# Four attention layers: a new step form for layer 4, reordered loads at each layer's head, moved splits in the middle loops

## The reference, cut to what matters

```python
x = layer0(x, ctx)   # 8 heads of 128: self attention, norm, cross attention, norm, feed-forward, norm
x = layer1(x, ctx)   # 16 heads of 16: self attention (mask), cross attention, feed-forward, three norms
x = layer2(x, ctx)   # as layer1, other mask and weights
# layer3:
q = (x @ Wq.T + bq).reshape(B, 128, 16, 16)
k = (ctx @ Wk.T + bk).reshape(B, 128, 16, 16)
v = (ctx @ Wv.T + bv).reshape(B, 128, 16, 16)
att = softmax(einsum('bhqd,bhkd->bhqk', q, k) / sqrt(16))
out = x + (einsum('bhqk,bhkd->bhqd', att, v) @ Wo.T + bo)
out = layer_norm(out) * gamma + beta
```

## Time and profile before

| | us |
|---|---|
| median of 3 runs | 3384.29 (3381.09 to 3385.19) |
| the profiled execution | 3386.52 |
| its span | 3384.8 |
| PE busy | 3052.0 |
| DVE busy | 2036.9 |
| ACT busy | 1909.7 |
| POOL busy | 1491.7 |
| SP's first load of cross / middle / fourth | 615.29 / 1454.23 / 3021.05 |

### The profile page before, as it was taken

The page is one execution under the profiler, slowest core; times in us unless marked ns, Lnnn a source line. Parts: engine busy times, 40 slices in busy tenths (PEclk is TensorE's granted clock), DMA queues, the critical chain, the costliest instruction groups (busy, mean ns, idle before and its releaser), DMA issues. The chain is left out here.

```text
span 3384.8 us, 82099 instructions
## 1 busy us (share of the span) xinstructions
PE 3052.0 (90%) x28400; PEld 2668.3 (79%) x28400; DVE 2036.9 (60%) x4306; ACT 1909.7 (56%) x7826; POOL 1491.7 (44%) x1874
## 2 busy tenths in 40 slices
PE   7999999599999999727999999999999999848886
PEld 5999998379999999625888888888888888745664
DVE  2545554244444444325777777888878778726665
ACT  2444444234444444325777777777777777617775
POOL 1223423103445444611555555555555555543444
PEclk8999999799999999858999999999999999979998
DMA  3222121410111110032222222333211121122321
GB/s 104 63 75 68 62 93 38 143 35 29 54 53 53 53 35 28 35 117 82 77 74 71 73 73 70 91 95 111 64 61 61 61 62 56 33 81 83 88 88 57
DMA packets 218094, 232.77 MB, mean 69 GB/s; under 512 B 41920, under 2 KB 183232, under 8 KB 215360
## 3 DMA queue, kind: packets, MB, share of 16 engines
q1 hardware_dynamic: 217920, 230.49, 21.6%
HBM read 148.57 MB, written 65.01 MB: 63 GB/s over the span
## 5 line engine op out<-in xcount | busy, mean ns | idle before, releaser
L1736 ACT ACTIVATE middle_stage<-middle_psum,middle_neg_max 128x128 f32<-128x128 f32 x2048 | 728.0, 392 | 344.6 <-DVE middle_neg_max L1716 344.4
L1736 ACT ACTIVATION_READ_ACCUMULATOR middle_stage<-middle_psum,middle_neg_max 128x1 f32 x2048 | 473.4, 231 | 0.0
L1716 DVE TENSOR_REDUCE middle_neg_max<-middle_psum 128x4 f32<-128x512 f32 x512 | 338.1, 682 | 64.9 <-PE middle_psum L1679 63.2
L1690 PE MATMUL middle_psum<-middle_eye,middle_stage 128*128 128x128 f32 x2048 | 320.5, 279 | 18.6 <-DVE middle_stage L1722 8.6
L1690 PEld LDWEIGHTS middle_psum<-middle_eye,middle_stage 128*128 128x128 f32 x2048 | 231.2, 142 | 72.0 <-issue 46.4
L1645 POOL TENSOR_TENSOR middle_attended_lo<-middle_mix,middle_attended_hi 128x256 fp32r<-128x256 f32 x128 | 95.0, 742 | 433.9 <-DVE middle_attended_hi L1728 433.9
L536 POOL TENSOR_TENSOR cross_ff_hidden_lo<-cross_ff_relu,cross_ff_hidden_hi 128x256 fp32r<-128x256 f32 x128 | 100.9, 789 | 279.9 <-DVE cross_ff_hidden_hi L531 279.9
L97 PE MATMUL middle_psum<-middle_n_yt_hi,middle_w_lo 128*128 128x256 f32 x640 | 193.7, 303 | 14.1 <-ACT middle_n_y L1853 12.5
L1946 POOL TENSOR_TENSOR middle_ff_hidden_lo<-middle_ff_relu,middle_ff_hidden_hi 128x256 fp32r<-128x256 f32 x256 | 183.4, 737 | 49.0 <-DVE middle_ff_hidden_hi L1940 49.0
L1722 DVE COPY middle_stage<-middle_psum 128x512 f32<-128x512 f32 x256 | 175.6, 686 | 15.6 <-PE middle_psum L1690 15.3
L1617 ACT ACTIVATE fourth_stage<-fourth_psum,fourth_neg_max 128x128 f32<-128x128 f32 x512 | 182.1, 387 | 3.4 <-DVE fourth_neg_max L1593 3.4
(11 more groups left out here) (346 smaller groups left out, 10915.8 us busy)
## 6 DMA issues: line engine op xcount, KB each, us to landing
middle_stage<-middle_a_k SPq DMA_DIRECT2D x1024, 16.0 KB, 1.8
middle_xt_hi<-x_hi SPq DMA_DIRECT2D x32, 256.0 KB, 2.7
middle_xt_lo<-x_lo SPq DMA_DIRECT2D x32, 256.0 KB, 3.0
middle_ct_hi<-context_hi SPq DMA_DIRECT2D x32, 256.0 KB, 2.9
middle_ct_lo<-context_lo SPq DMA_DIRECT2D x32, 256.0 KB, 3.2
middle_x_rows<-x_rows SPq DMA_DIRECT2D x32, 256.0 KB, 2.8
middle_mask_flags<-flags SPq DMA_DIRECT2D x128, 64.0 KB, 1.9
x_rows<-middle_n_z SPq DMA_DIRECT2D x32, 256.0 KB, 2.2
```

Of the source, the lines that this page charges most:

```text
L1690: ins = pe.transpose(banks.psum[:, TURN_BANK, x * SEQ:(x + 1) * SEQ], self.sh.p_wide[:, 4 * b + t, x, :], self.sh.eye[:])
L1716: dve.tensor_reduce(self.sh.neg_max[:, 4 * b + t, :], psum[:, SCORE_BANKS[t], :].rearrange("p (x k) -> p x k", x=4), AX_X, ALU.max, negate ...
L1736: ins = act.activation(self.sh.p_wide[:, 4 * b + t, x, :], psum[:, SCORE_BANKS[t], x * SEQ:(x + 1) * SEQ], ACT.Exp, bias=self.sh.neg_max[: ...
```

## The change

In words. (1) `phase8`: SP loads the first fold's operands, p_turned before arena, then the columns; v_row and rows come later. PE waits for the columns only ahead of its first bias sum and later for `bias_sums_read` in place of `biases`. In self ACT splits x(0) after the first fold, and POOL does its x split ahead of its wait for `biases`. In cross the two feed-forward pieces go to a buffer of their own (`late`, on y_rows and z2) and are split in round 0 behind heads 3 and 5. (2) Heads of the 16-head phases: the first piece is cut in two halves of 1024 columns; x, columns and further pieces are loaded in the order of need; in middle ACT splits pieces 0 and 1, copies k and q, then splits the rest; each k is spread as soon as its block is cleared. (3) Middle's loops: norm 2's high part is made by DVE, ACT's spread of x1 moves behind the exponentials of group 3, and DVE's norm of x1's first batch moves behind the last turned copy. (4) `phase16_last` uses `AttendWide`: one batch's sixteen heads at a time, in half steps; high parts by DVE; k is projected and spread two steps ahead; x, context are loaded three steps ahead, v's product goes to `FF_BANK`.

```diff
@@ phase8, SP
-            sp.dma_start(col[:], cols).then_inc(small_loaded.sem, 16)
-            sp.dma_start(v_row[:], v_row_dram.broadcast_to([P, H8 * DK8])).then_inc(small_loaded.sem, 16)
-            sp.dma_start(row[:].rearrange("p n f -> p (n f)"),
-                         rows.rearrange("(o n) f -> o (n f)", o=1).broadcast_to([P, len(names) * DM])) \
-              .then_inc(small_loaded.sem, 16)
             for i in range(n_big):
                 if i == 2:
+                    sp.dma_start(v_row[:], v_row_dram.broadcast_to([P, H8 * DK8])) \
+                      .then_inc(row_table_loaded.sem, 16)
...
                     load_round(0)
-                if 2 <= i < 5:
+                if 2 <= i < 4:
                     sp.wait_ge(folded.sem, i - 1)
-                elif i >= 5:
-                    sp.wait_ge(lo_made.sem, 4 * 3 + i - 4)
+                elif i == 5:
+                    sp.wait_ge(lo_made.sem, 14)
                 at = 3 * 512 + i * STAGE_COLS
-                half = slice((i % 2) * STAGE_COLS, (i % 2 + 1) * STAGE_COLS)
-                sp.dma_start(stage[:, half], packed[:, at:at + STAGE_COLS]) \
-                  .then_inc(stage_loaded[i].sem, 16)
                 if i < 3:
                     sp.dma_start(inner[:, i % 2, :], packed[:, i * 512:(i + 1) * 512]) \
                       .then_inc(stage_loaded[i].sem, 16)
+                sp.dma_start(staged(i), packed[:, at:at + STAGE_COLS]) \
+                  .then_inc(stage_loaded[i].sem, 16)
+                if i == 0:
+                    sp.dma_start(col[:], cols).then_inc(cols_loaded.sem, 16)
@@ phase8, ACT and DVE, one_round
+                    if cross and not post and h in (3, 5):
+                        weight_hi(4 + (h - 3) // 2)
...
+                    if cross and not post and h in (3, 5):
+                        weight_lo(4 + (h - 3) // 2)
@@ phase8, PE
-            pe.wait_ge(small_loaded.sem, 16 * 3)
...
-            pe.wait_ge(biases.sem, 1)
+            pe.wait_ge(bias_sums_read.sem, 1)
@@ phase8, POOL
-            pool.wait_ge(biases.sem, 1)
...
             make_flags(0)
+            pool.wait_ge(biases.sem, 1)
             one_round(0, False, False, True)
@@ phase16_full, ACT, x1
                     norm2.act(act, Back(r, 2), psum)
-                    norm2.act_hi(act, Back(r, 2))
-                spread(x1)
                 exp(x1_next, 2)
...
                 exp(x1_next, 3)
+                spread(x1)
@@ phase16_full, ACT, head
-            act.wait_ge(layer.lo_made.sem, layer.slots)
+            for s in range(2):
+                layer.act_piece(act, s)
+            act.wait_ge(layer.biases.sem, 1)
             proj1.act_k(act, 0, psum)
             proj1.act_q(act, 0, psum)
+            for s in range(2, layer.slots):
+                layer.act_piece(act, s)
+            act.wait_ge(layer.lo_made.sem, layer.slots)
@@ phase16_full, DVE, x1
                 if ok(-2):
+                    norm2.dve_hi(dve, Back(r, 2))
                     norm2.dve_lo(dve, Back(r, 2))
+                turned(x1[1], 3)
                 norm(x1[0])
-                turned(x1[1], 3)
@@ phase16_last, SP
-                    after, before, loaded = near(r, i, 1), near(r, i, -2), near(r, i, 2)
-                    if after:
-                        after[0].proj.sp_k(sp, after[1])
+                    keys, loaded, before = near(r, i, 2), near(r, i, 3), near(r, i, -2)
                     if loaded:
-                        loaded[0].sp_context(sp, loaded[1], ctx_t, tokens(r, i, 2))
-                        loaded[0].sp_x(sp, loaded[1], x, tokens(r, i, 2))
+                        loaded[0].sp_x(sp, loaded[1], x, tokens(r, i, 3))
+                    if keys:
+                        keys[0].proj.sp_k_chunk(sp, keys[1], 0)
+                    if loaded:
+                        loaded[0].sp_context(sp, loaded[1], ctx_t, tokens(r, i, 3))
+                    if keys:
+                        keys[0].proj.sp_k_chunk(sp, keys[1], 1)
+                        keys[0].sp_rows(sp, keys[1], x, tokens(r, i, 2))
@@ phase16_last, PE, one step
+                    if here:
+                        here[0].att.pe_scores(pe, here[1], banks, 1)
+                    turn(here, 0, 0)
+                    if before:
+                        before[0].att.pe_mix(pe, before[1], banks, 1)
+                    turn(here, 0, 1)
+                    if after:
+                        project_q(after)
+                    turn(here, 0, 2)
+                    turn(here, 0, 3)
+                    if before:
+                        before[0].att.pe_out(pe, before[1], banks, before[0].norm.sum_ready)
+
+                    if after:
+                        after[0].att.pe_scores(pe, after[1], banks, 0)
+                    turn(here, 1, 0)
+                    if keys:
+                        project_k(keys)
+                    turn(here, 1, 1)
+                    if here:
+                        here[0].att.pe_mix(pe, here[1], banks, 0)
+                    turn(here, 1, 2)
+                    if after:
+                        after[0].proj.pe_v(pe, after[1], banks, after[0].ct)
+                    turn(here, 1, 3)
@@ phase16_last, DVE, first half of one step
+                    inverse(here, 0)
+                    maximum(here, 1, 0)
+                    turned(here, 0, 0)
+                    maximum(here, 1, 1)
+                    norm(before, 1)
+                    turned(here, 0, 1)
+                    maximum(here, 1, 2)
+                    maximum(here, 1, 3)
+                    turned(here, 0, 2)
+                    turned(here, 0, 3)
```

404 lines of the change are left out of this document (207 added, 197 removed).

## The result

The changed kernel takes 3374.03 us (median of 16 runs), the kernel before 3384.62 (16 runs): ratio 0.9968, 95% interval 0.996 to 0.9976. It is faster, by 10.6 us (0.3%). The forecast was 3330, 3304 to 3357, so the direction came true and the size did not: a fifth of the expected 54 us. The profiled execution of the changed kernel took 3374.15 us.

What follows compares the result with a forecast made beforehand. Bounds: idle PE at the heads, PE in middle's loops, a chain across engines in fourth's. Terms -8.9 - 3.9 - 20 + 5 - 26.7 = -54.5 from 3386.5 give 3332.0, less 2.2: 3329.8, said 3330; range 3304 to 3357.

Steps and rivals of the forecast that it cites:

- Fourth's term, -26.7: Fourth's head and loop: 0.7 us gained at the head, 26 in the loop by shorter steps of two batches.
- Self's head, -8.9: Start of self: first fold 4 us sooner by load order, attention 4.7 us sooner by POOL's earlier x split.
- Cross's head, -3.9: Start of cross: 9 us off the head, 5.2 us added in round 0 by the moved weight splits.
- The 4 us at the fold: Start of cross: first fold's operands loaded first, so the fold was to start 4 us sooner, as in self.
- The two terms of the swap: Cross's feed-forward splits moved into round 0: idle 5.01 us off the head, 5.2 us added in round 0.
- Middle's head, -20: Start of middle: halved first piece, earlier x and k copy bring the first scores near 1481 in place of 1501.7.
- Middle's loops, +5: Middle's rounds: PE's 0.72 us wait for ACT goes, a 1.1 us wait for DVE's copy comes; layer 1 cancels.
- Rival (a): Middle's loops: norm and moments fit in DVE's idle times, -21 us in place of +5, total 3304; chance 0.2.
- The step of 18.1: Fourth's loop: a wide step of two batches takes 18.1 us in place of 19.98, bound by ACT's chain.
- my SP chain: Fourth's loop: SP's 16 DMAs with two loads between land 17.8 us into the step, so SP nearly binds.
- rival (c): Fourth's loop: less busy PE loses its clock, each step +5 us or more, total 3426; chance 0.05.
- rival (b): Fourth's loop: the wide step is no faster, as reading PSUM isn't sped up; total 3356; chance 0.15.

Runs made afterwards that it cites:

- experiment 4: Changed kernel with the starting semaphore increments of each phase dealt out to PE, ACT and POOL in thirds: 3361.9 us, 0.9933 of the kernel before.
- m_spread_only: Changed kernel with norm 2's high part in middle put back on ACT, late spread and norm kept: 3395.0 us, 1.0024 of the kernel before.
- f_store_early: Changed kernel with fourth's store of two steps back issued by SP ahead of k's spread: 3371.3 us, 0.9951 of the kernel before.
- experiment 7: Changed kernel with cross's two feed-forward pieces split before round 0 again, new load order kept: 3376.0 us, 0.9968 of the kernel before.
- m_all_back: Changed kernel with middle's loop order put back (high part on ACT, spread and norm at old places): 3352.8 us, 0.991 of the kernel before.
- m_hi_only: Changed kernel with middle's spread and DVE's norm put back, norm 2's high part kept on DVE: 3332.6 us, 0.9838 of the kernel before.
- combo3: Changed kernel with middle's spread and norm put back, starting increments shared by PE, ACT and POOL, fourth's store ahead of k's spread: 3313.2 us, 0.9783 of the kernel before.

## Why the prediction was wrong, step by step

**The step that failed most.** Fourth's term, -26.7, came at -7.4: its loop was taken to be bound by ACT's chain alone, and falls of PE's clock, SP's store and a longer head and tail had no price in it. The second is middle's, -20 + 5 together, where PE's start and the chain to the maximum were wrong: +6.6. The direction came true, the size only by a fifth.

**Self's head, -8.9: -8.3 measured, in part for other reasons.** The fold started at 9.59 and not 4 us sooner, at 6.7; experiment 4 shows that PE's increments held it, since with a third of them it starts at 6.46. POOL's split off the path came true: attention starts 5.8 us sooner, at 49.0. The other 2.5 us lie elsewhere, and a difference of this size says little. Self is the same code in eight of the profiled kernels, and took 602.0 to 613.1 us. Most of that is there at the first maximum already, at 54.18 us in the shortest (`m_spread_only`) and 62.08 in the longest (`f_store_early`); the time between the later maxima is the same to 0.2 us. What differs in the head is the clock. The window from 30 to 62 us in the shortest, the longest, the changed kernel and the kernel before:

```profile
30.00:62.00 32.00, 29.37 (x148) 21.11 (x149) 14.37 (x22) 8.89 (x18) 5.27 (x5) 1.00 0.22 74
```

```profile
30.00:62.00 32.00, 30.43 (x124) 19.67 (x124) 11.80 (x18) 7.27 (x10) 0.00 (x0) 0.89 0.16 58
```

```profile
30.00:62.00 32.00, 30.50 (x135) 21.12 (x134) 12.69 (x20) 8.04 (x17) 2.46 (x4) 0.89 0.16 58
```

```profile
30.00:62.00 32.00, 25.86 (x97) 16.77 (x96) 9.25 (x14) 6.72 (x9) 6.87 (x3) 0.79 0.18 57
```

So the same code at the same place had the clock at 1.00 or at 0.89, and -8.3 and -3.2 of single executions can't be told from values some us away.

**Cross's head, -3.9: -3.2, by luck.** The 4 us at the fold didn't come: its first matmul stands 9.67 us after SP's first load and stood 9.82 before, with 63 increments ahead of it. The two terms of the swap were both too small and cancelled: I had 5.0 off the head and 5.2 into round 0, and experiment 7 shows 11.2 and 8.6.

**Middle's head, -20: -15.2.** The first maximum comes 33.4 us after the first load (48.6 before), and I said 28 to 29. (My own terms, 1463 + 4 + 10.1 + 1.8, add up to 1478.9 and not to the 1481 that I wrote.) The failed step is "lets PE begin near 1463", 8.8 us after the first load: x landed in time, but PE was at its increments until 14.26 us in. I had read the idle time before PE's first matmul as a wait for the DMA that ended last. 3.8 us more were lost before the first store of x; with the loop's order put back (`m_all_back`) 2.3 of them are gone.

**Middle's loops, +5: +18.** The mechanism, its place and both instructions were right: the norm waits for the spread, and PE's turn waits for the copy. The mis-sized term is the chain to the maximum. I had 1.1 us of wait; it is 1.6 in layer 2. DVE's casts of the hidden part are two, 0.80 us here (I took 0.41, which two took before), and the norm starts 0.19 after the scores where I had 0.04. And in layer 1 I let it cancel against the mask's matmuls, though they stand ahead of the scores and so move with them: PE waits 1.2 us a round there. Rounds are +0.4 us in layer 1 and +0.75 in layer 2, which with the rounds between the layers makes +18.0 from the first to the last store of x. Rival (a), in which the gain is kept, is refuted for this order; `m_hi_only` keeps it by leaving the spread in its place.

**Fourth, -26.7: -7.4.** The step of 18.1 exists: 18.3, the chain of ACT with one wait for the spread. Three terms were missing. The ring: my SP chain ended with the last landing of k at 17.8 us and left out the store behind it, its landing and the bank that the sum holds. The clock: rival (c) named it at 1 in 20 and priced it as all or nothing; it came in part, four falls in these 13 steps of 1.5 us each. With rival (c)'s own figures I judged 8.5 of 10 busy to be safe because 8.8 had been; at 8.2 to 8.6 the rows show 0.96 to 0.98. And head and tail, which I had at -0.7 and 0, cost +4.4 and +2.7, since a wide first batch waits for all of k and a wide last one leaves more to do after its exponentials. Of rival (b), the rule on reading PSUM: the step did fall, 19.9 to 18.96, so it doesn't hold it at 19.98, but of the expected 26 us the loop brought 14.4. The missing 19 us are accounted for nearly in full: falls 6.0, ring 1.8, head 5.1, tail 2.7, and 0.2 in each of 14 steps (18.3 for 18.1) 2.8. One bound of this term had a slip too: 14 steps of 19.2 come to -11 by its own working, not -8.

**The range** failed because its upper end took one rival at a time; the terms of middle's loops (+13), fourth (+19) and middle's head (+5) failed together.

## What to carry to other kernels

When PE's idle time before the first matmul of a phase has the same length whatever is loaded, look for instructions that the profile doesn't count as busy: here 57 to 92 semaphore increments. If an instruction is moved to give its engine time, follow who reads its result: the 0.8 us that ACT saved became 1.2 to 1.6 us of PE's wait, while half of the same edit was pure gain. And a loop with little slack to the clock's fall can be made faster by useless matmuls in PE's waits, here by 8.5 us of 351; a change that only takes work off PE may pay part of its gain back in clock. Last, when two terms of a forecast cancel, read both sides in the trace: cross came out right with neither side right.

## What the runs showed of the hardware that I had not expected

- A semaphore increment issued by PE takes an estimated 0.154 to 0.155 us (9.67 us for 63, 14.26 for 92, 12.57 for 81, 8.79 for 57). Shared with ACT and POOL, PE's first matmul came 3 to 8 us sooner.
- In fourth's loop PE was busy 70 to 73 of 85 us in the changed kernel and in `combo3`, and the clock read 0.96 to 0.98; with 0.8 us of repeated matmuls per step (`c3_fill`) PE was busy 74 to 75 and the clock read 1.00. Each fall cost 1.5 us.
- The same code took 602 to 613 us for self in different executions; 7.9 us of it arose before the first maximum, where the clock read 1.00 in one and 0.89 in the other.

The best kernel here, `c3_fill`, takes 3308.6 us, 0.976 of the kernel before. It has the change's heads, cross and wide step and the high part on DVE, without the late spread, and with the shared start, the store moved and the repeated product.
